# Score units and side steps of an attention and expert kernel share one pool of four PSUM banks

## The reference

```python
x = _layernorm(x + _L0_attn_ref(x, w_qkv, w_out, head_scales))
x = _layernorm(x + _L0_ffn_ref(x, ...))

# _L0_attn_ref: 8 heads of 16, causal, a rank-1 term added to the scores
scores = jnp.einsum('bhqd,bhkd->bhqk', q, k) * scale
scores = jnp.where(causal[None, None], scores, -jnp.inf)
scores = scores + head_scales[None, :, None, None] * geo
attn = jax.nn.softmax(scores, axis=-1)
out = jnp.einsum('bhqk,bhkd->bqhd', attn, v).reshape(B, T, C)
return out @ w_out

# _L0_ffn_ref
x = x + mla_attention(rmsnorm(x, norm1_w), ...)   # 16 heads of 8, latent of 64, rotated q and k, causal
x = x + moe(rmsnorm(x, norm2_w), ...)             # all 4 experts of 512 hidden, one picked by argmax of the gate
```

## Time and profile before

| | us |
|---|---|
| median of 3 runs | 676.39 (674.8 to 678.23) |
| profiled execution, its own time | 673.76 |
| its span in the profile | 671.9 |
| TensorE busy | 582.0 (87%) |
| VectorE busy | 413.1 (61%) |
| ScalarE busy | 337.8 (50%) |

### The profile page before, as it was taken

The page is one execution under the profiler, slowest core; times in us unless marked ns, Lnnn a source line. Parts: engine busy times, 40 slices in busy tenths (PEclk is TensorE's granted clock), DMA queues, the critical chain, the costliest instruction groups (busy, mean ns, idle before and its releaser), DMA issues.

```text
span 671.9 us, 10096 instructions
## 1 busy us (share of the span) xinstructions
PE 582.0 (87%) x3668; PEld 279.0 (42%) x3717; DVE 413.1 (61%) x1031; ACT 337.8 (50%) x621; POOL 145.5 (22%) x186
## 2 busy tenths in 40 slices
PE   5578899958777877879999999999989999799994
PEld 3224233424223233424433344455544545357663
DVE  3496987796615968897778878754566402422313
ACT  4234457544463454557766667545546555633330
POOL 7612112313371031135321214011012011101000
PEclk9798899978787998999999999999999999989997
DMA  4856020000044020031313030220000000000000
GB/s 141 210 159 219 26 73 25 2 1 0 32 116 75 1 65 0 3 64 48 85 28 60 6 65 0 31 35 1 2 0 18 2 0 1 17 0 1 17 1 16
DMA packets 27394, 27.69 MB, mean 41 GB/s; under 512 B 6289, under 2 KB 22545, under 8 KB 27090
## 3 DMA queue, kind: packets, MB, share of 16 engines
q1 hardware_dynamic: 26962, 26.26, 16.2%
q0 software_dynamic: 384, 0.79, 0.5%
HBM read 19.40 MB, written 7.34 MB: 40 GB/s over the span
## 4 chain that ended last, share of the span: by engine, by line
PE 64%; DVE 20%; DMA 4%; issue 4%; ACT 4%; POOL 2%; SPq 1%; DVEq 0%; ACTq 0%; POOLq 0%
PE ps L875 13%; PE ps L948 10%; PE ps L858 10%; DVE mparts L1238 10%; PE ps L837 9%; PE ps L1004 8%; PE ps L834 3%; PE ps L937 3%; PE ps L931 2%; ACT pr L1024 2%; DMA qs<-nparts 2%; PE ps L912 2%; PE ps L946 2%; PE ps L886 1%; DVE stats L1147 1%
## 5 line engine op out<-in xcount | busy, mean ns | idle before, releaser
L1024 ACT ACTIVATE pr<-ps 128x512 f32<-128x512 f32 (+1 forms) x456 | 250.3, 576 | 227.9 <-PE ps L858 192.1
L1238 DVE TENSOR_REDUCE mparts<-ps 128x1 f32<-128x512 f32 (+3 forms) x456 | 279.9, 655 | 112.4 <-PE ps L837 111.2
L837 PE MATMUL ps<-ks,qs 125*128 125x512 bf16 (+3 forms) x576 | 170.0, 337 | 12.6 <-DVE mparts L1238 11.1
L858 PE MATMUL ps<-qs,ks 128*128 128x512 bf16 (+3 forms) x532 | 154.6, 332 | 15.7 <-ACT pr L1024 9.2
L752 POOL TENSOR_SCALAR_AFFINE_SELECT pr<-pr 128x512 f32<-128x512 f32 x96 | 61.0, 636 | 369.1 <-ACT pr L1024 368.9
L875 PE MATMUL ps<-pr,vs 128*32 128x512 f32 (+3 forms) x1152 | 126.4, 512 | 0.4 <-POOL pr L752 0.4
L858 PEld LDWEIGHTS ps<-qs,ks 128*128 128x128 bf16 x576 | 50.8, 99 | 143.2 <-ACT pr L1024 92.5
L834 PE MATMUL ps<-cmask,identb 128*128 128x128 bf16 (+2 forms) x259 | 64.9, 251 | 26.9 <-DVE mparts L1238 12.5
L837 PEld LDWEIGHTS ps<-ks,qs 125*128 125x128 bf16 x576 | 55.4, 100 | 53.1 <-DVE mparts L1238 21.2
L948 PE MATMUL ps<-w,work 128*128 128x128 f32 x512 | 74.1, 288 | 0.0
L1089 ACT ACTIVATE work<-ps,b 128x512 f32<-128x512 f32 x64 | 43.8, 686 | 49.1 <-PE ps L1004 48.5
(11 more groups left out here) (119 smaller groups left out, 391.5 us busy)
## 6 DMA issues: line engine op xcount, KB each, us to landing
qs<-scr1q SPq DMA_DIRECT2D x64, 64.0 KB
ks<-scr1k SPq DMA_DIRECT2D x64, 64.0 KB
qs<-scr0q SPq DMA_DIRECT2D x48, 64.0 KB, 2.3
ks<-scr0k SPq DMA_DIRECT2D x36, 64.0 KB, 2.2
scr0q<-parts SPq DMA_DIRECT2D x4, 384.0 KB, 2.8
scr0k<-parts SPq DMA_DIRECT2D x4, 384.0 KB, 3.2
scr1q<-parts SPq DMA_DIRECT2D x4, 384.0 KB, 2.5
scr1k<-parts SPq DMA_DIRECT2D x4, 384.0 KB, 2.6
```

The source lines that it names most:

```text
L837: last = pe.matmul(bank[:, h, :], queries(F, KMAX, h0 + h, i * P, P), ks[0:KMAX, F % SLOTS, h0 + h, 512 * c:512 * c + w], start=not diagon ...
L858: last = pe.matmul(to[:, h, :], ks[0:KEXP, F % SLOTS, h0 + h, j * P:(j + 1) * P], queries(F, KEXP, h0 + h, qb * 512 + lo, n), start=True, ...
L1024: act.activation(pr[:, st % PSLOTS, h0:h0 + nh, 0:STEPS[st][3]], scores_at(F, v), ACT.Exp, scale=GROUPS[F][0].scale).then_inc(exped, 1)
L1238: dve.tensor_reduce(mparts[:, F % SLOTS, h0:h0 + nh, i, c], maxes_at(F, u), AX_X, ALU.max).then_inc(taken, 1)
```

## The change

Score units lose their own two banks. `plan()` now gives a bank to each score unit too, by the same rule as to side steps, from one pool of banks 0 to 3 (with bank 4 until the first `pv`). A unit waits for whoever reads what lay in that bank: the exponential of an earlier unit, or the reader of a side step. The order of the steps is the same on every engine, and so is every instruction; only bank addresses and waits differ.

```diff
-SCB, SCN = 0, 2
-SIDE = [2, 3]
+SHARED = [0, 1, 2, 3]
...
-    banks, nth_use = [0, 1, *SIDE, PVB], {}
+    banks, nth_use = [*SHARED, PVB], {}
...
-        if kind == "scores" and s[1] == 0 and s[2] < SCN:
-            banks = SIDE
-            freed_by[s] = reader[SCB + s[2]]
-        elif s == ("pv", 0, 0):
+        if s == ("pv", 0, 0):
+            banks = SHARED
             freed_by[s] = reader[PVB]
...
-        elif kind in READER or kind == "proj":
+        elif kind in READER or kind in ("proj", "scores"):
             bank = min((b for b in banks if b not in reader or reader[b] in nth), key=lambda b: nth_use.get(b, -1))
             nth_use[bank] = len(nth)
...
-            if kind == "proj":
+            if kind == "scores":
+                reader[bank] = s
+            elif kind == "proj":
...
-            bank = ps[:, SCB + (F * NU + v) % SCN, 0:nh * STEPS[s][3]]
+            bank = side("scores", F, v)[:, 0:nh * STEPS[s][3]]
...
-                    pe.wait_ge(done[reader[0]], nth(*reader))
+                    pe.wait_ge(exped if reader[0] == "scores" else done[reader[0]], nth(*reader))
...
-                if F or v >= SCN:
-                    pe.wait_ge(exped, nth("scores", F, v) - SCN)
```

## The result

| | before | after |
|---|---|---|
| median, us | 675.6 (671.74 to 678.23, 4 runs) | 688.39 (686.55 to 693.64, 4 runs) |
| profiled execution, its own time | 673.76 | 686.55 |
| its span | 671.9 | 684.7 |
| mean granted clock | 0.954 | 0.963 |

The ratio is 1.0196, with an interval of 1.016 to 1.0232: the change makes the kernel some 13 us slower. A later set of six runs gave 1.0197 (1.0161 to 1.0233).

What follows compares the result with a forecast made beforehand. Up to 300 us the chain passes through VectorE and transfers, afterwards TensorE's full in-order queue bounds. 12.7 + 1.6 + 4.2 - 1.2 - 7.3 = +10.0 us on the 676.39 median gave 686.4 us, range 678.4 to 694.

Steps and rivals of the forecast that it cites:

- eight waits for `pick_up`: Between 449 and 568 us, score units get an expert's bank that `pick_up` on VectorE still has to read: +12.7 us.
- `pick` and the hidden layer: After the gate, score units wait for both picks, while the first hidden layer gets another bank and comes sooner: +1.6 us.
- projections, rotation, the others: After 300 us, new waits for rotations, latent features, value copies, the residual and relu: +4.2 us.
- taken back behind the fourth `pick_up`: A transpose at 500.17 us had waited 1.19 us for VectorE; TensorE arriving later takes that back: -1.2 us.
- waits for the exponential that go: After 300 us, 30 score-unit waits for the exponential two units back vanish, all counted as gained: -7.3 us.
- the start, up to 300 us: Gains and new waits both end at VectorE steps and loads that don't move: 0, bounds 4 us faster, 3 us slower.
- half of the 7.3 us turned into the next wait: Allowance in the range's upper end: 3.6 us of the removed exponential waits after 300 us is met again.
- seven of the eight: `pick_up` has a maximum in front on VectorE, wait over a microsecond; at 555.67 the queue was empty, wait 0.28 us.
- The last 72 us: After the step "quiet" no score unit is left, so this end should be as long as before.
- It cancels: Rival: stalls let VectorE and ScalarE catch up, half of 18.5 us goes, leaving +2 us, 678.4 us; chance 0.13.
- The rotation pays: Rival: short exponential waits go and `pick_up` readers are in time, 9 us faster, 667 us; chance 0.07.
- The clock follows: Rival: repeated 2 us idles lower the granted clock over 450 to 600 us, costing about 10 us, 697 us; chance 0.05.

Runs made afterwards that it cites:

- experiment 2: Kernel before, banks as they were, with eight score units made to wait for the `pick_up` that the changed kernel makes them wait for: 688.43 us, ratio 1.0175.
- Experiment 5: Changed kernel with bank age counted from the reader's place in the order, plus extra steps for readers on VectorE: 668.26 us, ratio 0.9906.
- experiments 6 and 7: `turn` of five groups two steps later: with four banks, reader-counted age and late readers, 668.17 us, ratio 0.9893; in the kernel before, 677.23 us, ratio 1.0013.
- experiments 1 and 3: To the changed kernel: bank age counted from its reader, 673.14 us, ratio 0.9945; or the expert's bank marked used again at `pick_up`, 680.0 us, ratio 1.0044.
- experiment 4: Changed kernel, with eight `pick_up` steps put right behind the expert's last block in VectorE's order alone: 684.41 us, ratio 1.01.
- experiments 2 and 8: The first: eight `pick_up` waits added to the kernel before, 688.43 us; the second: the changed kernel timed again as it was, 688.56 us.
- experiment 7: Kernel before, two banks for scores, with the `turn` of groups 5, 6, 8, 9 and 10 two steps later: 677.23 us, ratio 1.0013.

## Why the prediction was right, and where not

I forecast 686.4 us, 678.4 to 694, slower with 0.81. It came out at 688.39. For the profiled execution I had +10.0 us, and it was +12.8. That the median is only 2.0 us off is in part luck: behind 300 us the trace lost 13.7 us, the start happened to be 0.9 us ahead, and the kernel before came out 0.8 us under the median that I had added to. By its own terms, measured against the kernel before step by step:

| term | forecast, us | measured, us |
|---|---|---|
| eight waits for `pick_up` | +12.7 | +12.96 |
| `pick` and the hidden layer | +1.6 | +1.3 |
| projections, rotation, the others | +4.2 | +5.0 |
| taken back behind the fourth `pick_up` | -1.2 | -0.9 |
| waits for the exponential that go | -7.3 | -7.65, of which 3.3 came back |
| the start, up to 300 us | 0 | -0.9 |
| sum | +10.0 | +12.8 (the lines add to 13.1) |

**The step that was mis-sized** is "I count all 7.3 us as gained". The waits went, 7.65 us of them, but about 3.3 us turned into the next wait on TensorE's queue: six `turn` steps of groups 5 to 7 waited 0.45 us for `evac` where they had waited 0.30 (0.94 us in all), and towards the end, beside group 11, `y`, `pv` and two `feed` steps lost 0.3 to 0.7 us each. That these belong to the waits that went, and not to the stalls, shows in experiment 2: it has the stalls and keeps the short waits, and there the same steps lose nothing. I had this in the range ("half of the 7.3 us turned into the next wait"), not in the sum. Experiment 5 shows the same with no wait for `pick_up` or `pick` (7.5 us removed, 3.1 gained), and experiments 6 and 7 show that such a wait has hardly a price of its own.

**The mechanism** was right: the bank taken longest ago is not the one freed longest ago. Experiment 2 puts the eight waits into the old kernel and loses 11.9 us by the medians, 13.3 behind 300 us in the traces; experiments 1 and 3 take them out of the new one, and the loss goes or shrinks to 3.4 us. The durations, read from the old trace alone, hold to within 0.3 us in all (12.7 against 12.96): VectorE's queue around a `pick_up` is the same, and TensorE's arrival was known. One reading behind them was wrong: not seven of the eight have work in front of `pick_up` on VectorE, but six. At the sixth VectorE's queue was empty as at 555.67, and the wait was 1.18 us against 0.29 there; an empty queue is not enough, TensorE must also have work before its next score unit, as it has at the seventh.

**The other small waits** were 0.8 us dearer than the 4.2 us: relu with 1.15 us and the value copy with 0.61 are late more often than the old trace let me see. **The last 72 us** are as long as before: the lag is 12.8 us at 600 us and at the end.

**It cancels**: refuted by experiment 2. Of 13.5 us of stall 1.25 came back at the transpose, and hardly anything elsewhere.

**The rotation pays**: not with this rule for age. `pick_up` at once behind its block (experiment 4) still leaves 5.17 us, as the read takes 1.12 us itself. With the right age it does pay, 0.9945 and 0.9906, though less than the 9 us I had given it. The Trainium skill ("Perfetto Trace Analysis", Optimizing Tensor Performance, Matmuls) asks for independent groups in different banks so that their evacuation overlaps. The traces agree for banks that were in truth free, and show that a bank of another number whose reader is still due is worse than the same bank again.

**The clock follows**: not in the profiled execution of the result, and a little in others. There the granted clock from 300 to 600 us was 1.00, and that of the kernel before 0.99, with TensorE busy 11 us less, first the changed kernel, then the one before:

```profile
300.00:600.00 300.00, 274.13 (x1880) 131.02 (x1876) 175.43 (x405) 171.55 (x321) 54.40 (x75) 1.00 0.11 23
```

```profile
300.00:600.00 300.00, 285.24 (x1901) 136.84 (x1926) 177.47 (x417) 177.53 (x330) 54.41 (x75) 0.99 0.11 23
```

The 0.93 from 550 to 600 us, which I took as a sign for this rival, was one interval at half clock (586.5 to 593.3 us), and it only moved on with the work (599.6 to 606.4). But three traces have the eight long waits, and two of them, experiments 2 and 8, have 3.4 us at half clock right behind one of the longer waits, at a cost of 1.1 and 1.6 us; the clock is 0.97 from 500 to 550 us there. In the eight others, the first trace of the changed kernel among them, it is 1.00 in each 50 us from 300 to 550. The place suggests that the long waits bring it; that is not shown, and what decides whether it comes, no run tried. The size of the rival, 10 us, was wrong by far.

## What to carry to other kernels

When banks go round by age, count the age from the step that frees the bank, and add what its engine is usually late by; a bank held over several steps but marked at the first is otherwise handed out just as its reader starts, and on an engine whose queue is in order everything behind waits too. Price each wait that a change adds from the reader's end in the old trace: on the engine that bounds the kernel nearly the whole of a 1 to 2 us wait is kept (all but 1.25 of 13.5 us). Don't book the waits of a few tenths that it removes at their sum: here 3.3 of 7.65 us, and some 4.4 of 7.5 in experiment 5, came back at waits behind.

## What the runs showed that I had not expected

**The first 320 us vary.** The last rotation starts at 318.75 us before, at 322.97 in experiment 7, whose order is nearly the same up to there, and at 320.46 and 324.72 in two executions of the changed kernel. That is the stretch in which VectorE and transfers bound, and in which the granted clock lies between 0.90 and 0.94. From there to the first `pick` it is 106.27 and 105.92 us in the first two, 104.93 and 104.87 in the others: what differs arose earlier. The runs of one kernel spread over 4 to 9 us, so it took a dozen of them to tell 3 us. The time goes with the granted clock: of the 42 runs of the kernel before in the two sets, the 18 with a mean clock of 0.947 or less took 677.9 us on average, the 21 with 0.952 or more 674.6. What sets either is open; no run here tried it. The differences between medians in experiments 1 and 3, 3.4 us each, are no larger than this; the traces behind 300 us agree in sign and nearly in size (2.35 us gained and 3.0 lost).

**The row of the waits overstates.** The weight loads' 92.5 us for exponentials still stand at 57.0 us in the version that is 7.3 us faster. Worked out step by step the matmuls' own waits of this kind add up to about 15 us over the whole kernel before, as the prediction had it (7.3 and 7.9 us).
